# Attention inner loop of a two-layer transformer kernel: the order of score, maximum and value matmuls within a step

## The reference

```python
q, k, v = heads(norm(x) @ Wq.T), heads(norm(x) @ Wk.T), heads(norm(x) @ Wv.T)
scores = einsum('bhqd,bhkd->bhqk', q, k) * scale      # layer 1 adds a causal mask and rotates q and k
probs  = softmax(scores)                              # layer 0 then mixes in a copy without key 0
out    = einsum('bhqk,bhkd->bhqd', probs, v) @ Wo.T + bo
```

## Time and profile before

| what | us |
|---|---|
| median of 3 runs (lowest, highest) | 2335.18 (2333.16, 2338.78) |
| the profiled execution's own time | 2329.27 |
| its span, first to last instruction | 2326.7 |
| TensorE matmul busy | 2085.1 (90%) |
| VectorE busy | 1621.4 (70%) |
| ScalarE busy | 1334.7 (57%) |
| GpSimd busy | 519.9 (22%) |
| mean granted TensorE clock, share of full | 0.953 |

### The profile page before, as it was taken

One profiled execution on the slowest core, in us unless ns is written; L12 is line 12 of the kernel. 1 busy time (PEld: TensorE's weight loads), 2 busy tenths in 40 slices (PEclk: granted clock), 3 DMA queues, 4 the chain that ended last, 5 costly groups with the idle time before them and its releaser, 6 DMA issues. The chain is left out here.

```text
span 2326.7 us, 45876 instructions
## 1 busy us (share of the span) xinstructions
PE 2085.1 (90%) x17861; PEld 1304.2 (56%) x17861; DVE 1621.4 (70%) x2087; ACT 1334.7 (57%) x2564; POOL 519.9 (22%) x567
## 2 busy tenths in 40 slices
PE   4999689999999999859969998839999999987998
PEld 3887533333333333348858887615555555546888
DVE  7776499999999999246774447947777777716433
ACT  3443258888888888604434553306667677652444
POOL 2000321211321411440021113762221212112110
PEclk9999879999999999979979999958999999999999
DMA  4004732433534442110030001693444545310000
GB/s 137 1 0 172 236 58 43 72 75 58 107 63 86 79 81 51 51 45 1 0 115 1 0 0 64 195 183 66 80 92 80 102 94 101 67 53 19 28 18 27
DMA packets 124765, 162.76 MB, mean 70 GB/s; under 512 B 55321, under 2 KB 78617, under 8 KB 124569
## 3 DMA queue, kind: packets, MB, share of 16 engines
q1 hardware_dynamic: 107352, 120.72, 24.3%
q0 software_dynamic: 17216, 39.37, 6.3%
HBM read 95.04 MB, written 63.70 MB: 68 GB/s over the span
## 5 line engine op out<-in xcount | busy, mean ns | idle before, releaser
L1460 DVE TENSOR_REDUCE att_maxes<-att_s_max 128x2 f32<-128x1024 f32 (+2 forms) x832 | 973.9, 1183 | 189.0 <-PE att_s_max L1281 88.5
L1439 ACT ACTIVATE att_probs<-att_s_exp 128x512 f32<-128x512 f32 (+3 forms) x1792 | 888.0, 552 | 242.5 <-PE att_s_exp L1338 117.4
L1362 PE MATMUL att_o_ps<-att_probs,att_v_st 128*32 128x256 f32 (+1 forms) x6912 | 526.3, 376 | 14.9 <-ACT att_o_sb L1418 14.2
L1338 PE MATMUL att_s_exp<-att_q_st,att_k_st 64*128 64x512 f32 (+3 forms) x1792 | 459.5, 474 | 4.4 <-ACT att_probs L1439 3.9
L1298 PE MATMUL att_s_max<-att_k_st,att_q_st 62*128 62x512 f32 (+3 forms) x1792 | 395.6, 418 | 69.0 <-POOL att_k_st L1508 33.3
L1338 PEld LDWEIGHTS att_s_exp<-att_q_st,att_k_st 64*128 64x128 f32 x1792 | 189.7, 184 | 343.1 <-ACT att_probs L1439 295.0
L1362 PEld LDWEIGHTS att_o_ps<-att_probs,att_v_st 128*32 128x32 f32 x6912 | 138.0, 108 | 256.8 <-issue 140.5
L1298 PEld LDWEIGHTS att_s_max<-att_k_st,att_q_st 62*128 62x128 f32 x1792 | 189.2, 194 | 92.4 <-issue 56.6
L1533 POOL TENSOR_TENSOR att_m_parts<-att_m_turned,att_zeros 32x128 fp32r<-32x128 f32 x64 | 28.9, 451 | 530.1 <-ACT att_m_turned L1405 390.3
L587 DVE TENSOR_TENSOR ffn1b_h_lo<-ffn1b_h,ffn1b_h_hi 128x512 fp32r<-128x512 f32 x64 | 45.0, 704 | 111.0 <-PE ffn1b_acc L135 99.2
L1546 POOL DMA_DIRECT2D attention_rows<-att_o_sb x64 | 37.5, 586 | 358.6 <-ACT att_o_sb L1418 358.6
(11 more groups left out here) (296 smaller groups left out, 3997.7 us busy)
## 6 DMA issues: line engine op xcount, KB each, us to landing
att_q_st<-q_parts SPq DMA_DIRECT2D x384, 64.0 KB, 5.2
att_k_st<-k_parts SPq DMA_DIRECT2D x192, 128.0 KB, 4.9
attention_rows<-att_o_sb POOLq DMA_DIRECT2D x64, 256.0 KB, 3.8
output_wide<-attention_weights POOLq DMA_DIRECT2D x48, 256.0 KB, 5.2
q_parts<-qkv_parts SPq DMA_DIRECT2D x16, 512.0 KB, 3.8
k_parts<-qkv_parts SPq DMA_DIRECT2D x16, 512.0 KB, 2.7
v_rows<-qkv_vt SPq DMA_DIRECT2D x16, 512.0 KB, 4.5
att_v_raw<-v_rows SPq DMA_DIRECT2D x32, 256.0 KB, 6.3
```

Source lines behind the costliest of these rows:

```text
L1338: mm = pe.matmul(s_exp[:, plan.bank[place], q0:512], k_st[rows, it.set, pr, kt * P:(kt + 1) * P], q_st[rows, it.set, qc, pr, q0:512], star ...
L1362: mm = pe.matmul(o_ps[j * VW:(j + 1) * VW, cols], v_st[:, it.par, kt, j, :], probs[:, step % 2, j, cols], start=kt == 0 and part == 0, sto ...
L1439: act.activation(probs[:, step % 2, j, q0:512], s_exp[:, plan.bank[place], q0:512], ACT.Exp, scale=1.0 if causal else 0.25).then_inc(s["ex ...
L1460: v.tensor_reduce(maxes[:, qc, :, pairs, qt - 4 * qc, kc], banks, AX.X, ALU.max).then_inc(s["max_done"], 1)
```

## The change

The two slots of a step become one. The order on TensorE is now: score pair 0, 1; all units of the step; score pair 2, 3; the value matmuls of the step before over all its queries at once (a matmul of up to 512 columns for each head in place of two of up to 256); the turns of the step. The places in the ring follow that order: the four scores, then the turns. `RING` and `MBUFS` stay 3 and 2. VectorE and ScalarE follow the same order.

```diff
-SLOTS = 2
...
-        self.feed = [between(lead + at_s[i] + (at_s[i + 1] - at_s[i]) * n // SLOTS,
-                             lead + at_s[i] + (at_s[i + 1] - at_s[i]) * (n + 1) // SLOTS)
-                     for i in range(self.NS) for n in range(SLOTS)]
+        self.feed = [between(lead + at_s[i], lead + at_s[i + 1]) for i in range(self.NS)]
...
         for i in range(self.NS):
-            for n in range(SLOTS):
-                for j in (2 * n, 2 * n + 1):
-                    self.place["step", i, j] = len(users)
-                    users.append(("step", i, j))
-                for d, what, a in self.feed[i * SLOTS + n]:
-                    if what == "turn":
-                        self.place["turn", a] = len(users)
-                        users.append(("turn", a))
+            for j in range(GH):
+                self.place["step", i, j] = len(users)
+                users.append(("step", i, j))
+            for d, a in self.turns(i):
+                self.place["turn", a] = len(users)
+                users.append(("turn", a))
...
-    def slots(self, step):
-        return self.feed[step * SLOTS:(step + 1) * SLOTS]
+    def units_of(self, step):
+        return [(d, a) for d, what, a in self.feed[step] if what == "unit"]
+
+    def turns(self, step):
+        return [(d, a) for d, what, a in self.feed[step] if what == "turn"]
...
-                def values(it, step, part, first):
+                def values(it, step, first):
...
                     for j in range(GH):
-                        mm = pe.matmul(o_ps[j * VW:(j + 1) * VW, cols], v_st[:, it.par, kt, j, :], probs[:, step % 2, j, cols],
-                                       start=kt == 0 and part == 0, stop=step + 1 in plan.begin, skip_group_check=True)
-                    if part == 1:
-                        mm.then_inc(s["pv_done"], 1)
+                        mm = pe.matmul(o_ps[j * VW:(j + 1) * VW, q0:512], v_st[:, it.par, kt, j, :], probs[:, step % 2, j, q0:512],
+                                       start=kt == 0, stop=step + 1 in plan.begin, skip_group_check=True)
+                    mm.then_inc(s["pv_done"], 1)
...
-                        for n, slot in enumerate(plan.slots(step)):
-                            for j in (2 * n, 2 * n + 1):
-                                scores(it, step, j, first)
-                            feed(it, slot)
-                            if step > 0:
-                                values(it, step - 1, n, first)
-                            elif not first:
-                                values(it.ahead(-1), NS - 1, n, False)
+                        for j in range(GH // 2):
+                            scores(it, step, j, first)
+                        for d, a in plan.units_of(step):
+                            if it.ahead(d).exists:
+                                max_unit(it.ahead(d), a)
+                        for j in range(GH // 2, GH):
+                            scores(it, step, j, first)
+                        if step > 0:
+                            values(it, step - 1, first)
+                        elif not first:
+                            values(it.ahead(-1), NS - 1, False)
+                        for d, a in plan.turns(step):
+                            place = plan.place["turn", a]
+                            turn_max(it.ahead(d), a, place, plan.bank[place], plan.in_use(it, place))
...
-                        for n, slot in enumerate(plan.slots(step)):
-                            for j in (2 * n, 2 * n + 1):
-                                place = plan.place["step", step, j]
-                                act.wait_ge(s["st_ready"], plan.pieces(it, place, 1))
...
-                            feed(it, slot)
+                        for j in range(GH):
+                            place = plan.place["step", step, j]
+                            act.wait_ge(s["st_ready"], plan.pieces(it, place, 1))
...
+                        for d, a in plan.turns(step):
+                            place = plan.place["turn", a]
+                            copy_max(it.ahead(d), a, plan.pieces(it, place, 1), plan.bank[place])
```

More of the change, by code:

```diff
@@ L984, in __init__ @@
         all_s, all_u = sum(cost_s), sum(cost_u)
-        total = all_s * all_u * SLOTS
-        at_s = [sum(cost_s[:i]) * all_u * SLOTS for i in range(self.NS + 1)]
-        at_u = [sum(cost_u[:i + 1]) * all_s * SLOTS for i in range(self.NU)]
+        total = all_s * all_u
+        at_s = [sum(cost_s[:i]) * all_u for i in range(self.NS + 1)]
+        at_u = [sum(cost_u[:i + 1]) * all_s for i in range(self.NU)]
         at = [(at_u[a], ("unit", a)) for a in range(self.NU)]
@@ L1314, in turn_max @@
                     pe.transpose(s_exp[0:KC * UROWS, bank, 0:P], neg_max[:, :], E.ident[:, :]).then_inc(s["st_ready"], 1)
[L1316 to L1323, removed]
                 def scores(it, step, j, first):
@@ L1344, in scores @@
                     mm.then_inc(s["st_ready"], 1)
-                def values(it, step, part, first):
+                def values(it, step, first):
                     qc, kt, q0 = plan.steps[step]
-                    middle = q0 + (512 - q0) // (2 * P) * P
-                    cols = (slice(q0, middle), slice(middle, 512))[part]
-                    if step == 0 and part == 0:
+                    if step == 0:
                         pe.wait_ge(s["v_ready"], it.n(1, 1))
@@ L1354, in values @@
                             pe.wait_ge(s["constants"], FILLS)
[L1355 to L1360, removed]
+                    pe.wait_ge(s["exp_done"], plan.pieces(it, plan.place["step", step, GH - 1], 1))
+                    if kt == 0 and not (first and qc == 0):
+                        pe.wait_ge(s["o_copied"], it.n(2, qc))
                     for j in range(GH):
-                        mm = pe.matmul(o_ps[j * VW:(j + 1) * VW, cols], v_st[:, it.par, kt, j, :], probs[:, step % 2, j, cols],
-                                       start=kt == 0 and part == 0, stop=step + 1 in plan.begin, skip_group_check=True)
-                    if part == 1:
-                        mm.then_inc(s["pv_done"], 1)
+                        mm = pe.matmul(o_ps[j * VW:(j + 1) * VW, q0:512], v_st[:, it.par, kt, j, :], probs[:, step % 2, j, q0:512],
+                                       start=kt == 0, stop=step + 1 in plan.begin, skip_group_check=True)
+                    mm.then_inc(s["pv_done"], 1)
                 pe.wait_ge(s["nm_zero"], 1)
@@ L1378, in body @@
                     for step in range(NS):
-                        for n, slot in enumerate(plan.slots(step)):
-                            for j in (2 * n, 2 * n + 1):
-                                scores(it, step, j, first)
-                            feed(it, slot)
-                            if step > 0:
-                                values(it, step - 1, n, first)
-                            elif not first:
-                                values(it.ahead(-1), NS - 1, n, False)
+                        for j in range(GH // 2):
[12 more added lines that the diff above has]
+                            turn_max(it.ahead(d), a, place, plan.bank[place], plan.in_use(it, place))
                 each_iteration(pe, body)
-                end = It(0, ITERS - 1)
-                values(end, NS - 1, 0, False)
-                values(end, NS - 1, 1, False)
+                values(It(0, ITERS - 1), NS - 1, False)
             choose(pe, path)
@@ L1405, in copy_max @@
                     act.activation(m_turned[:, :], s_exp[0:KC * UROWS, bank, 0:P], ACT.Copy).then_inc(s["exp_done"], 1)
[L1407 to L1411, removed]
                 def copy_out(it, qc):
@@ L1432, in body @@
                             copy_out(it, 0)
-                        for n, slot in enumerate(plan.slots(step)):
-                            for j in (2 * n, 2 * n + 1):
-                                place = plan.place["step", step, j]
-                                act.wait_ge(s["st_ready"], plan.pieces(it, place, 1))
[L1437 to L1440, removed]
-                            feed(it, slot)
+                        for j in range(GH):
+                            place = plan.place["step", step, j]
+                            act.wait_ge(s["st_ready"], plan.pieces(it, place, 1))
+                            if j == 0 and (not first or step >= 2):
+                                act.wait_ge(s["pv_done"], it.n(NS, step - 1))
+                            act.activation(probs[:, step % 2, j, q0:512], s_exp[:, plan.bank[place], q0:512], ACT.Exp,
+                                           scale=1.0 if causal else 0.25).then_inc(s["exp_done"], 1)
+                        for d, a in plan.turns(step):
+                            place = plan.place["turn", a]
+                            copy_max(it.ahead(d), a, plan.pieces(it, place, 1), plan.bank[place])
                 each_iteration(act, body)
@@ L1476, in turned @@
```

(7 more changed lines are left out.)

## The result

The changed kernel is slower: 2364.2 us, the median of four runs (2357.0 to 2374.9), against 2334.2 (2331.8 to 2338.8) for the kernel before; the ratio is 1.013, with a 95% interval of 1.0084 to 1.0176. A second series on another chip gave 2363.3 (2354.8 to 2373.4) against 2333.5, a ratio of 1.0143 (1.0117 to 1.0169). The profiled execution took 2368.8, with a span of 2367.0; the second series' 2354.8, with a span of 2353.0.

A forecast was written before the change was run, and what follows sets the result against it. TensorE was taken to pace the kernel, VectorE 0.07 behind. Layer 0 at +21 to +22 us and layer 1 at +1 made +22 on the 2335.2 median, forecast 2357.5; 8-in-10 range 2343 to 2373.

The forecast's parts named there:

- The ring wait (c): Layer 0 step: fourth score waits for the first score's bank, 1.18 after the first load; step 2.62 instead of 2.48.
- TensorE's chain (a): Layer 0 step: two of four array shape changes go, so TensorE's own work takes 2.13 in place of 2.48.
- VectorE (b): Layer 0 step: VectorE's two reductions at 1.17 each would stop TensorE's gain at 2.34.
- The copy (d): Layer 0 steps copying `o_ps`: only delays the first exponential by 0.04; saves 0.31, twice an iteration.
- The turn (e): Layer 0 steps with a turn: costs 0.21, half of the old 0.43; saves 0.22, twice an iteration.
- Its chain over GpSimd and SyncE: Work following a turn: starts about 1 us later, costed at nothing, or 1 us an iteration if its cover were gone.
- groups of steps: Layer 1 iteration: steps 0 to 4, 5, 6 and 7 to 11; sum 31.21, before 31.27.
- the predicted +2 in the last two iterations: Layer 1's last two iterations, short of units, lose about +2, what layer 0's last loses.
- the clock as a rival: Layer 1 steps 3 to 5 fall to a lower clock, some 1.5 us each: +24 more, 2381; chance 0.06.

The follow-up runs named there:

- Experiment 2: The kernel before with only the value matmuls merged, at the end of the second slot, one unit still behind each score pair; 2457.2 us.
- experiment 3: Small extra ScalarE operation ahead of the first exponential of each layer 0 step: 2386.7 us in the changed kernel, 2344.0 us in the kernel before.
- experiment 4: The changed kernel with VectorE reducing only the first half of each unit's keys, output wrong; 2341.6 us.
- with filler: The changed kernel with unread extra matmuls in place of the missing units in layer 1's last iteration; 2356.0 us, second series 2357.8 us.

## Why the prediction was right, point by point

**The ring wait (c)** was the forecast's centre and held: 1.19 + 0.42 + 1.00 = 2.61 against 1.18 + 0.44 + 1.00 = 2.62. Experiment 2 ties the wait to the merged values, experiment 3 to the first exponential, and experiment 4 takes VectorE out.

**TensorE's chain (a) and VectorE (b)**, 2.13 and 2.34, lie under 2.61 and were never reached in any run; the first stays an estimate. That VectorE isn't the bound of the changed layer 0 is shown. In the Trainium skill, TensorEngine Tiling (Array Packing), § Key Properties says that changing the tiling mode drains TensorE. By that alone the kernel would have gained. § PSUM Bottleneck of the same page of the Trainium skill says that tiling does not speed up the evacuation of PSUM, and that the copy may become the bottleneck once TensorE is four times as fast. The trace agrees as to the place of the wait: the fourth score waits 0.31 us with no weight load running, for a bank that ScalarE has not yet read. But it is the delay of one evacuation and not ScalarE's throughput, for ScalarE itself idles 0.54 a step.

**The copy (d)** was sized at 0.04 and cost 0.08 (steps 0 and 1 of layer 0 take 5.30, where 2 x 2.61 is 5.22). **The turn (e)** cost 0.21, as predicted: steps 3 and 4 take 5.43. Its chain over GpSimd and SyncE stayed hidden. An iteration of layer 0 took 42.33, predicted 42.40 (the terms as written add up to 42.42), and the layer +21.6, predicted +21 to +22. That the layer's sum came out so well is in part luck: 15 iterations at +1.1 and the last at +3.6 make 20.1. The other 1.5 lie in the first iteration, of which 8.4 us were at half clock instead of 5.1; the kernel of experiment 4, with 5.3 us at half clock there, does not have them.

**Layer 1** by groups of steps: predicted 11.63, 3.07, 3.86 and 12.65, measured 11.61, 3.09, 3.85 and 12.62. The step with three units was the only place where a shorter reduction shortened the iteration. Layer 1's +1.9 of the second profile has the predicted +2 in the last two iterations (+2.2), +2.0 in the first, of which 8.1 us were at half clock instead of 3.8, and -2.3 in the thirteen between.

**The total.** The forecast was 2357.5 (2335.2 + 22 is 2357.2) and the median 2364.2: 30.0 above the kernel before, where the forecast had 22.3. The second profile, whose clock held in the attention of layer 1 behind its first iteration, has a span 26.3 above the one before, of which the two attentions are 23.4 (21.5 and 1.9). Another 2.3 lie ahead of layer 0, which starts anywhere from 315.0 to 320.3 in the profiles of either order. Of the some 8 us by which the median missed, 5.5 go with the clock: in the second series the median without filler is 29.8 above the kernel before, and 24.3 with filler. The other 2 have no cause shown and lie within the spread of the runs.

I had the clock as a rival with a chance of 0.06 and in the wrong place: steps 3 to 5 of every iteration, from the one fall of the earlier trace rows. The same row pointed at a place where the long fall then came, the last iteration. It should have stood in the forecast as a cost of some 5 to 10 us in a part of the executions, and not as a separate story. That the change has a part in it, by taking work from TensorE there, is argued and not shown.

## What to carry to other kernels

Count the users of a ring of buffers between two blocks of other work, and not only their mean rate: with three banks, the fourth in a row waited for one whole score-to-exponential latency (1.19 us here), and merging the work that stood between them exposed it. The latency to compare with is read from starts (load to exponential, exponential, release), and a trace often has one place where the wait already shows. Where steps differ in width, choose the order step by step; the gain of a change that nets to nothing over an iteration can be had without its losses.

## What the runs showed of the hardware that I had not expected

A kernel with less idle time in its distances can look less busy, and the reverse: TensorE was "49.17 busy" in 50 us at 1.24 a half step, and "50.00" at 1.305. Its records overlap and their ends are modelled.

The same work took one iteration a third longer in one execution than in another, and more work did not. With 203 weight loads (204 in the second record) in the last iteration it took 37.7 and 28.4, at a mean granted clock of 0.66 and 1.00; with 253 it took 28.6. In the longer one the clock stayed at half until the attention ended, 25.9 us on, although TensorE's records covered 24.9 of them.
